# Attention and expert block: candidates of the key search from two x ranges instead of indices, centred output weights, gates in weights, and small softmax steps on GpSimd

## What is computed

```
x = x + layernorm(attn(layernorm(x)) @ w_o.T)
x = x + layernorm(ffn(layernorm(x)))

attn: q, k, v = h @ w_q.T, h @ w_k.T, h @ w_v.T;  sq, sk = elu(q) + 1, elu(k) + 1
      memory_output = active * (sq @ memory) / clip(sq @ memory_norm)
      local_output  = causal linear attention in chunks of 128, with a running state S, z
      out = g * memory_output + (1 - g) * local_output          # g = sigmoid(gate)

ffn:  dense   = silu(h @ W_up.T) @ W_down.T                     # inner size 1024
      scores of 4 heads against 64 x keys and 64 y keys; top 8 of each side
      all sums x + y of these 8 x 8; the best 8 of them; index = 64 * ix + iy, held to 1023
      w = silu((h . down_embed[index]) * softmax(best 8));  experts = sum of w * up_embed[index]
```

## Time and profile before

| | us |
|---|---|
| median of 3 runs | 3796.57 (3795.65 to 3799.4) |
| the profiled execution | 3794.85 |
| its span, from the first to the last instruction | 3793.1 |
| busy DVE | 3336.2 (88%) |
| busy PE | 3206.2 (85%) |
| busy ACT | 2280.8 (60%) |
| busy POOL | 2217.5 (58%) |
| mean granted clock of TensorE | 0.966 |

### The profile page before, as it was taken

How to read it: one execution, slowest core, us unless ns; L and a number is a source line. 1 busy time by engine, 2 the same in 40 slices (tenths; PEclk the granted TensorE clock), 3 DMA queues, 4 the chain that set the end, 5 groups by cost and what they waited for, 6 DMA issues and landing times.

```text
span 3793.1 us, 68981 instructions
## 1 busy us (share of the span) xinstructions
PE 3206.2 (85%) x16506; PEld 2518.3 (66%) x16506; DVE 3336.2 (88%) x8582; ACT 2280.8 (60%) x3478; POOL 2217.5 (58%) x2069
## 2 busy tenths in 40 slices
PE   6888888888888888888888888888888888888886
PEld 4666666666666666666666666666666666666665
DVE  3998988889898898989889898898889889888896
ACT  3665656666566666666666666665666656666664
POOL 2665665566566555656555666566556556665563
PEclk8999999999999999999999999999999999999998
DMA  2333333333333333333333333333333333333332
GB/s 74 69 64 61 68 62 63 58 69 64 61 65 62 64 61 68 65 61 61 66 64 61 64 65 62 60 69 63 62 60 67 64 61 67 62 65 58 69 61 57
DMA packets 95972, 241.27 MB, mean 64 GB/s; under 512 B 8659, under 2 KB 46548, under 8 KB 95956
## 3 DMA queue, kind: packets, MB, share of 16 engines
q0 software_dynamic: 53248, 201.34, 29.4%
q1 hardware_dynamic: 42708, 39.73, 3.4%
HBM read 22.94 MB, written 16.78 MB: 10 GB/s over the span
## 4 chain that ended last, share of the span: by engine, by line
issue 34%; DVE 32%; POOL 17%; PE 11%; DVEq 3%; ACT 1%; DMA 1%; POOLq 1%; SPq 0%; ACTq 0%
POOL var_eps L319 8%; POOL rstd L321 6%; PE bank L444 5%; DVE picked L700 5%; PE bank L423 4%; DVE stats L675 4%; DVE top L724 4%; DVE prob L708 3%; DVE x_key L734 2%; POOL x_out L368 2%; DVE mv L680 1%; DVE xn L684 1%; DVE x_mid L851 1%; DVE sig L766 1%; DVE cand_best L740 1%
## 5 line engine op out<-in xcount | busy, mean ns | idle before, releaser
L329 POOL TENSOR_TENSOR sums<-scores 128x1024 f32<-128x1024 f32 x512 | 1243.4, 2442 | 787.0 <-ACT scores L605 787.0
L700 DVE SCALAR_TENSOR_TENSOR picked<-sums,cand_best,down 128x1024 f32<-128x1024 f32 x512 | 827.3, 1637 | 0.7 <-ACT down L574 0.7
L585 ACT ACTIVATE prob<-sums,neg_max 128x1024 f32<-128x1024 f32 x512 | 594.9, 1163 | 310.0 <-POOL sums L329 310.0
L708 DVE SCALAR_TENSOR_TENSOR prob<-picked,rz,prob 128x1024 f32<-128x1024 f32 x512 | 679.4, 1348 | 0.0
L319 POOL TENSOR_TENSOR var_eps<-mv,ln_eps 128x1 f32<-128x1 f32 x512 | 346.2, 676 | 509.1 <-DVE mv L680 509.1
L568 ACT ACTIVATE wexp<-prob 128x1024 f32<-128x1024 f32 x512 | 526.5, 1054 | 0.2
L519 PE MATMUL bank<-xn2T,wupT 128*128 128x128 f32 x4096 | 479.7, 275 | 0.0
L423 PE MATMUL bank<-wdownT,hT 128*128 128x256 f32 x2048 | 465.3, 380 | 7.0 <-ACT y_sb L628 7.0
L519 PEld LDWEIGHTS bank<-xn2T,wupT 128*128 128x128 f32 x4096 | 469.1, 192 | 0.1
L423 PE MATMUL bank<-ue,gT 128*128 128x256 f32 x2048 | 465.5, 380 | 2.4 <-ACT gT L579 2.4
L423 PEld LDWEIGHTS bank<-ue,gT 128*128 128x128 f32 x2048 | 390.6, 191 | 110.3 <-issue 60.3
(11 more groups left out here) (122 smaller groups left out, 5823.7 us busy)
## 6 DMA issues: line engine op xcount, KB each, us to landing
wexp<-wexp POOLq DMA_DIRECT2D x128, 1024.0 KB, 8.0
wexp<-wexp POOLq DMA_DIRECT2D x128, 512.0 KB, 4.6
x_in<-_attn_hidden_states_dram SPq DMA_DIRECT2D x128, 128.0 KB, 2.0
out_dram<-x_out SPq DMA_DIRECT2D x128, 128.0 KB, 1.7
wexp<-in_L_ffn_W_up_dram SPq DMA_DIRECT2D x1, 1024.0 KB, 8.3
prob<-in_L_ffn_down_embed_dram SPq DMA_DIRECT2D x1, 1024.0 KB, 10.8
ue<-in_L_ffn_up_embed_dram SPq DMA_DIRECT2D x1, 1024.0 KB, 13.1
wexp<-in_L_ffn_W_down_dram SPq DMA_DIRECT2D x1, 1024.0 KB
```

The costliest lines, as they stand in the source:

```text
L329: nc.gpsimd.tensor_tensor(sums[:, k, :, :], scores[:, k, 0:XIN].unsqueeze(2).broadcast_to([P, XIN, NKEYS]), scores[:, HEADS + k, :].unsque ...
L585: nc.scalar.activation(prob[:, h, :], sums[:, h, :, :].rearrange("p x y -> p (x y)"), ACT.Exp, bias=neg_max[:, h:h + 1]).then_inc(s_prob, 1)
L700: nc.vector.scalar_tensor_tensor(picked[:, h % 2, :], sums[:, h, :, :].rearrange("p x y -> p (x y)"), best[:, h, TOP - 1:TOP], down[:, :], ...
L708: nc.vector.scalar_tensor_tensor(prob[:, h, :], picked[:, h % 2, :], rz[:, h:h + 1], prob[:, h, :], ALU.mult, ALU.mult).then_inc(s_zexp, 1)
```

## The change

- **Candidates.** `MAX8` now runs on three ranges for each head: x keys 0 to 15, x keys 16 to 63, and the 64 y keys, 12 instructions for 8. `cand` holds two sets of 28 sums, those of the low and those of the high x range; the best 8 are taken over 56. `x_key`, `clamped` and the passes of `cmask` with it are gone, since the second set is by itself what falls on expert 1023.
- **Moved to POOL.** The candidate sums (now four instructions), `neg_max`, `cdif`, the product of mask and exponentials (`cprob`), and `z_last`. The factor `down[:, LAST_IN:]` is now ACT's `scale` in the silu of `z_last`.
- **Layer norms o and y.** `w_o` (transposed), `up_embed` and `W_down` (transposed) are centred once in the setup, on DVE, so that the outputs have mean zero. The mean square comes from an ACT `Square` with an accumulator, on a row with one more column that holds the epsilon; POOL only takes the power. Subtraction and separate addition are gone: `x_mid` and `x_out` are one DVE pass each (scale and add), and `x_out` moves from POOL to DVE.
- **Gates** are multiplied into `wvo` and `mem_x` in the setup; `coef` is gone. `mix`'s memory part is an ACT copy with scale.
- **State.** `sig` is one DVE instruction; the matmul for the state has 258 columns, in two banks, and one DVE addition takes them.
- **Order.** PE does the memory product before the local one, and the state's product and W_down's product after the turn of `xn1`. POOL's order has the new steps between the `sums`. DVE takes the best candidates after `sig`, `xn1` ahead of the second `select`, and `select` of the third head ahead of `xn2`. ACT does `head_prob(0)` after `sk_nat`. The gate's matmul is the first of the setup.

The diff, cut to its core (POOL's body and the two stretches of DVE and ACT that carry the change):

```diff
@@ gpsimd
+            def power(n, t):
+                pool.wait_ge(s_veps[n], t + 1)
+                nc.gpsimd.tensor_tensor(rstd[:, n:n + 1], var_eps[:, n:n + 1], minus_half[:, :], ALU.pow).then_inc(s_rstd[n], 1)
...
+                    head_sums(0)
+                    pool.wait_ge(s_top, f + 1)
+                    wait(pool, s_cm1, f)
+                    wait(pool, s_cdif, f)
+                    for kind in range(2):
+                        for cols, nb, x, y in pairs(top[:, kind, :, :], top[:, 2, :, :]):
+                            nc.gpsimd.tensor_tensor(
+                                cand[:, :, kind * NCAND + cols.start:kind * NCAND + cols.stop].rearrange("p h (a b) -> p h a b", b=nb),
+                                x, y, ALU.add).then_inc(s_cand, 1)
+                if g is not None:
+                    add_pairs()
+                if f is not None:
+                    pool.wait_ge(s_best, f + 1)
+                    wait(pool, s_prob, HEADS * f)
+                    nc.gpsimd.tensor_tensor(neg_max[:, :], zero[:, :], best[:, :, 0], ALU.subtract).then_inc(s_negm, 1)
...
+                    nc.gpsimd.tensor_tensor(cdif[:, :, :], cand_best[:, :, NCAND:], per_head(best[:, :, 0], NCAND + TOP),
+                                            ALU.subtract).then_inc(s_cdif, 1)
+                    head_sums(1)
+                if n is not None:
+                    inverse_std(LN_X, n)
+                if f is not None:
+                    head_sums(2)
                 if g is not None:
                     add_all()
+                if f is not None:
+                    head_sums(3)
                 if a is not None:
-                    inverse_std(LN_O, a)
...
-                    nc.gpsimd.tensor_tensor(x_out[:, :], x_mid[:, slot(h), :], ln_y[:, :], ALU.add).then_inc(s_out, 1)
+                    power(LN_O, a)
+                if f is not None:
+                    pool.wait_ge(s_cm1, f + 1)
+                    pool.wait_ge(s_cexp, f + 1)
+                    nc.gpsimd.tensor_tensor(cprob[:, :, :], cmask[:, :, :], cdif[:, :, 0:NCAND], ALU.mult).then_inc(s_pe, 1)
...
+                    nc.gpsimd.tensor_tensor(z_last[:, :].rearrange("p (h n) -> p h n", h=HEADS), cprob[:, :, :],
+                                            per_head(rz[:, :], NCAND), ALU.mult).then_inc(s_zlast, 1)
                 if a is not None:
                     inverse_std(LN_M, a)
+                if h is not None:
+                    power(LN_Y, h)
@@ scalar
+                if a is not None:
+                    act.wait_ge(s_mix, a + 1)
+                    nc.scalar.activation(mix_sq[:, :], mix[:, :], ACT.Square, scale=D ** -0.5,
+                                         accum_out=var_eps[:, LN_O:LN_O + 1]).then_inc(s_veps[LN_O], 1)
@@ vector
-                    for k in range(GROUPS):
-                        last = nc.vector.max(top[:, k, :], scores[:, k, :])
...
-                    for k in range(HEADS):
-                        last = nc.vector.max_index(x_key[:, k, :], top[:, k, :], scores[:, k, :])
...
-                    nc.vector.tensor_scalar(clamped[:, :, :], x_key[:, :, :], float(XIN), None, ALU.is_ge).then_inc(s_clamped, 1)
...
+                    for k in range(HEADS):
+                        nc.vector.max(top[:, 0, k, :], scores[:, k, 0:XIN])
+                        nc.vector.max(top[:, 1, k, :], scores[:, k, XIN:])
+                        last = nc.vector.max(top[:, 2, k, :], scores[:, HEADS + k, :])
...
+                    nc.vector.scalar_tensor_tensor(x_mid[:, slot(a), :], mix[:, 0:D], rstd[:, LN_O:LN_O + 1], x_in[:, slot(a), :],
+                                                   ALU.mult, ALU.add).then_inc(s_xmid, 1)
...
+                    nc.vector.scalar_tensor_tensor(x_out[:, :], y_sb[:, 0:D], rstd[:, LN_Y:LN_Y + 1], x_mid[:, slot(h), :],
+                                                   ALU.mult, ALU.add).then_inc(s_out, 1)
```

More of the change, by code:

```diff
@@ L89, in sandwich_kernel @@
         rstd = sb("rstd", [P, 4])
-        xn1, xn2, ln_o, ln_y, mix = (sb(n, [P, D]) for n in ("xn1", "xn2", "ln_o", "ln_y", "mix"))
+        xn1, xn2 = (sb(n, [P, D]) for n in ("xn1", "xn2"))
+        mix, mix_sq, y_sb, y_sq = (sb(n, [P, D + 1]) for n in ("mix", "mix_sq", "y_sb", "y_sq"))
         xn1T, xn2T = (sb(n, [P, DC, P]) for n in ("xn1T", "xn2T"))
@@ L375, in _ @@
         def _(pe):
[L376 removed]
+            pe.wait_ge(s_const, CONSTS)
             def setup_bank(n):
@@ L479, in body @@
                     last.then_inc(s_at_ps, 1)
-                    b = seq_of(a)
-                    pe.wait_ge(s_state, a + 1)
-                    pe.wait_ge(s_v, a + 1)
-                    for c in range(DC):
-                        nc.tensor.matmul(num_ps, sig[:, c, :], state[:, b, c, :], start=(c == 0), stop=False)
                     wait(pe, s_mix_mem, a)
@@ L510, in body @@
                     last.then_inc(s_xn1T_ps, 1)
+                if a is not None:
+                    pe.wait_ge(s_sk, a + 1)
+                    pe.wait_ge(s_mix_mem, a + 1)
+                    for c in range(DC):
+                        last = nc.tensor.matmul(ds_ps[:, c, :], sk_nat[:, c * P:(c + 1) * P], v_one[:, :],
+                                                start=True, stop=True)
+                    last.then_inc(s_ds_ps, 1)
+                if g is not None:
+                    wait(pe, s_y, g)
+                    pe.wait_ge(s_hT, 2 * g + 2)
+                    product(y_ps, IC, lambda c: hT[:, c, :], lambda c: wdownT[:, c, :], stop=False).then_inc(s_yh, 1)
                 if f is not None:
@@ L731, in body @@
-                    wait(dve, s_clamped, f)
+                    wait(dve, s_cand, 4 * f)
                     alone(dve)
                     for k in range(HEADS):
-                        last = nc.vector.max_index(x_key[:, k, :], top[:, k, :], scores[:, k, :])
-                    last.then_inc(s_xkey, 1)
-                    dve.wait_ge(s_cand, 2 * f + 2)
-                    wait(dve, s_sel, HEADS * f)
-                    alone(dve)
-                    for k in range(HEADS):
-                        last = nc.vector.max(best[:, k, :], cand[:, k, :])
@@ L790, in body @@
                 if f is not None:
-                    select(f, 1)
+                    dve.wait_ge(s_cexp, f + 1)
+                    wait(dve, s_rz, f)
+                    nc.vector.reduce_sum(zsum[:, :], cdif[:, :, NCAND:], axis=AX.X).then_inc(s_zsum, 1)
+                    select(f, 0)
+                    dve.wait_ge(s_zsum, f + 1)
+                    wait(dve, s_zexp, HEADS * f)
+                    wait(dve, s_zlast, f)
+                    nc.vector.reciprocal(rz[:, :], zsum[:, :]).then_inc(s_rz, 1)
                 if a is not None:
```

343 lines of the change are left out of this document (158 added, 185 removed).

## The result

The changed kernel takes 3542.43 us (median of 4 runs, 3540.66 to 3543.22). The kernel before took 3796.36 beside it. The ratio is 0.9329, with a 95% interval of 0.9313 to 0.9345: 254 us or 6.7% faster. The forecast was 3576, with a range of 3480 to 3695.

What follows compares the result with a forecast made beforehand. No engine is full: a chain through PE, ACT, DVE and POOL, the latter two taking turns, bounds the step. 28.93 less 27.15 us over 127 periods, 226 less 6, takes 3794.85 to 3575, median forecast 3576, range 3480 to 3695.

Steps and rivals of the forecast that it cites:

- The sum: Whole kernel: step from 28.93 to 27.15 us over 127 periods, 226 us, less 6 for fill and drain.
- The centring: Setup: passes over 512, 2048 and 2048 elements on an otherwise idle DVE, about 9.5 us, nothing booked.
- The clock: PE: clock drops behind 2.9 us of idle time, costing 0.81 us a step, 103 in all; taken to stay up.
- The rival that the clock still falls: PE: 0.8 to 1.2 us idle still lowers the clock every second step; about 3680 us, chance 0.15.
- Candidate sums: POOL, after the first `sums`: four sums at 0.3 us each, 1.2 together, bounds 0.8 and 2.9.
- POOL's and DVE's first half: Step from the first `MAX8` to the second `sums`, walked engine by engine, ending at 7.5 us.
- The turns: POOL and DVE from the first `select` on: passes alternate whole, second `weigh` ending at 17.0 us, `x_mid` following `cprob` at 18.05.
- `add_all` "costs nothing, though only just": POOL's DMA issue beside `select` and `weigh`: its wait for the first DMA, landed at 11.5 us, adds nothing.
- PE's wait for `xn2`: PE, late in the step: about 0.8 us of waiting, where it was 2.9.
- The rule on engine selection: Instructions moved to POOL: two-input elementwise work belongs on DVE, GpSimd about twice as slow; alone it predicts a loss.
- The rival of PE as the bound: Step falls to PE's 24.3 us plus 1.1 for `sig`, 25.4; about 3350 us, chance 0.09.

Runs made afterwards that it cites:

- `b_fill`: Kernel before the change, plus 16 idle turns of `ident` on PE in its idle gap ahead of `xn2`: 3697.72 us, ratio 0.9746.
- `a_ln_o`: Changed kernel with the statistics for the norm of o back on DVE, and `var_eps` and power on POOL, instead of ACT's `Square`: 3690.11 us, ratio 0.9725.
- `a_dve_idx`: Changed kernel with four index searches for the top y keys put back on DVE, behind the wait for ACT's exponential: 3747.46 us, ratio 0.9879.
- `a_pool_chain`: Changed kernel with one more POOL product of 128x112 between `cdif` and the second `sums`: 3679.49 us, ratio 0.9697.
- `a_soft_dve`: Changed kernel with `neg_max` and `cdif` back on DVE, ahead of `cmask`: 3436.17 us, ratio 0.9056.
- `a_best`: `a_turn_pe` with `neg_max` and `cdif` on DVE besides: 3334.22 us, ratio 0.8788.
- `a_turn_pe`: Changed kernel, same instructions, with another order on DVE and on PE: 3332.34 us, ratio 0.8787.
- `a_chain_tick`: `a_pool_chain` plus one POOL instruction of 4 elements between the third `sums` and the DMA issue `add_all`: 3579.84 us, ratio 0.9437.

## Why the prediction was right, point by point

- **The sum.** Forecast a gain of 220 us, measured 254. The step was forecast as 27.15 us and is 26.98: 127 times 0.17 is 22 us. The 6 us that I took back for shorter periods in the fill and drain aren't there: the mean over all 127, these included, is 26.98, and in the middle it is 27.00. The time outside the periods, booked at nothing with 2 us to either side, is 5.4 shorter, 2.5 of them in the setup and 2.9 behind the last copy. The centring was summed as 9.5 us; its own rate, 1.25 for 1024, gives 11.3, and the six passes take 10.5. Nothing was booked from it.
- **The clock.** Booked at 103 us, shown at 96 by `b_fill`. The rival that the clock still falls is refuted: it stays at 1.00 in the stretches shown, and its mean is 0.992. PE's idle times in a step were forecast as 1.1 for `sig`, 0.3 to 0.5 for the copy of y and 0.8 for `xn2`, and are 1.03, 0.18 and 0.52; 0.35 for `v_one` and 0.28 for `mix` were not forecast. The clock stays up in `a_ln_o` too, with 1.65 us of idle time for `xn2` and a mean of 0.992; in `a_dve_idx` it falls in every second step, behind 1.97 us.
- **Candidate sums.** Forecast 0.3 each, measured 0.298 and 0.272 (means of 256 each); the four take 1.01 us in a row, near the value taken and far from the upper bound of 2.9. The line between one element and 256 held. The DMA issue, 1.6 by the rows of before, took 1.15.
- **POOL's and DVE's first half.** `sig`, the best candidates, `neg_max`, `cdif` and the second `sums` end 4.3, 4.8, 5.2, 5.6 and 7.4 us behind the first `MAX8` (2005.99). Forecast were 4.25, 4.95, 5.15, 5.6 and 7.5.
- **`xn1` was mis-stated.** I let it run free beside the third `sums`. It is held by it: 1.91 us for 256 elements, where the same pass as `xn2` takes 0.41. This cost nothing only because the `select` behind it would have waited for the same turn.
- **The turns.** Forecast was `select` and first `weigh`, then the fourth `sums`. In fact the fourth `sums` came between them, and the first `weigh` took 2.92. The sum is the same, since the same three passes stand one after the other: the second `weigh` ends at 17.0, as forecast. The product `cprob` did go ahead of `x_mid`, whose start is 17.73 against 18.05. I had not seen this order coming, so that the sum is right is in part luck.
- **`add_all` "costs nothing, though only just".** This was the most sensitive term of the whole sum, more than I knew. It was 0.15 us late, and that gave `select` the turn. `a_pool_chain` shows 0.8 us a step hanging on it, over 100 us in all, and the order in the changed kernel is safe by some 0.12 us only; the forecast had no such term. That it came out right here is luck too.
- **PE's wait for `xn2`.** Forecast 0.8, measured 0.57. From `xn2`'s end to `MAX8` it is 5.03, unchanged. POOL's wait for the scores is 4.85 us a step, below 6.1, as forecast.
- **The rule on engine selection** ("GPSIMD Engine Reference", 4.1 Engine selection, in the Trainium skill) would have made the moved passes a loss. For `neg_max` and `cdif` the outcome agrees with it: `a_soft_dve` is 106 us faster. Its reason doesn't, since `neg_max` and `cdif` take 1.12 and 0.30 us on DVE and 0.28 and 0.43 on POOL; the gain is the earlier second `sums`, and in `a_best` the same move gains nothing. I had counted them as a loss within the sum, 1.85 us from the candidates to `cdif`, but not asked what the sum would be without it.
- **The rival of PE as the bound** had the right limit but not for this kernel: 25.4 us a step was its number, and `a_turn_pe` runs at 25.35. Even this is a near miss in kind: the number had PE's wait of 1.1 for `sig` in it, and `a_turn_pe` has none for `sig` but 1.6 for `hT`.

Open is how the 158 us outside the clock divide among the parts: `a_ln_o` gives 148 to the norm of o, `a_soft_dve` takes 106 away, and these don't add up, since each shifts the turns of the others.

## What to carry to other kernels

Time a DVE instruction spends behind a POOL instruction isn't work: find out who asked for the turn first before booking its removal, because the wait passes to the next instruction. Where two engines take turns, move the instruction that the chain needs to a place where it asks first, by 0.2 us if need be, and count a DMA issue on POOL as asking; `a_chain_tick` got 100 us that way. When a run comes out far from its forecast, look for such a change of order first. A new order alone, with the same instructions, brought 210 us more. And look at an idle stretch of PE of 2 to 3 us a step for its clock: filling one of 2.9 with idle turns brought 96 us without any change in the work.

## What the runs showed of the hardware that I had not expected

- A DVE `TENSOR_SCALAR` with only one SBUF tensor is held by a POOL instruction as well: `neg_max` took 2.19 us for 4 elements, and `xn1` of the changed kernel 1914 ns on average, where the same pass as `xn2` takes 413.
- 0.2 us in the order of asking decided 0.8 us a step, and one more POOL instruction of 0.24 us made a kernel 100 us faster. In `a_soft_dve` the order turned at a start 0.14 us behind that of POOL's DMA issue.
- Sixteen idle turns a step on PE made the kernel before 2.5% faster.
- A POOL instruction with two inputs takes some 200 ns for 1 element, 240 to 280 for 4, 298 for 64 and 430 for 112 (means of the changed kernel and of `tick`): up to 64 elements most of the price is fixed.
